# Attention on one core: VectorE adds the finished output projection to the result before it gates the next turn's first values

## The reference, cut to what matters

```python
q = _rope(jnp.einsum('bsd,hdp->bhsp', x, Wq))
k = _rope(jnp.einsum('bsd,hdp->bhsp', x, Wk))
gv = _gate(x, Wsel_v)                                   # sigmoid scores, the top 2 of 8 experts kept
v = jnp.einsum('bsd,bhse,hedp->bhsp', x, gv, Wv)
att = jax.nn.softmax(jnp.einsum('bhsp,bhtp->bhst', q, k) / np.sqrt(P), axis=-1)
o = jnp.einsum('bhst,bhtp->bhsp', att, v)
go = _gate(x, Wsel_o)
return jnp.einsum('bhsp,bhse,hepd->bsd', o, go, Wo)
```

## Time and profile before

| what | value |
|---|---|
| median of 3 runs | 3919.82 us (3918.64 to 3920.61) |
| the profiled execution's own time | 3914.3 us |
| its span, first to last instruction | 3912.5 us |
| mean granted TensorE clock, share of full speed | 0.980 |
| PE busy | 3596.8 us, 92% of the span |
| DVE busy | 3211.4 us, 82% |
| POOL busy | 2722.2 us, 70% |
| ACT busy | 2037.4 us, 52% |
| the sum into `acc`, 64 times | first starts at 1168.2 us, last at 3648.2 us |

### The profile page before, as it was taken

The page is one execution under the profiler, slowest core; times in us unless marked ns, Lnnn a source line. Parts: engine busy times, 40 slices in busy tenths (PEclk is TensorE's granted clock), DMA queues, the critical chain, the costliest instruction groups (busy, mean ns, idle before and its releaser), DMA issues. The chain is left out here.

```text
span 3912.5 us, 55524 instructions
## 1 busy us (share of the span) xinstructions
PE 3596.8 (92%) x15792; PEld 2472.4 (63%) x15792; DVE 3211.4 (82%) x3580; ACT 2037.4 (52%) x3795; POOL 2722.2 (70%) x2852
## 2 busy tenths in 40 slices
PE   6999999998669999999999999999999999999797
PEld 3444444444247777777777777777777777777586
DVE  6999989998748888888888887888887888888697
ACT  5666666666334454445454545444444445444455
POOL 4877788787657676677777677767677767776344
PEclk9999999999979999999999999999999999999898
DMA  2110111011043242323232323233323332222111
GB/s 78 54 49 27 65 70 71 20 56 60 25 159 81 56 110 55 81 60 105 55 87 78 77 64 100 60 76 89 76 60 77 88 73 68 66 70 68 43 33 49
DMA packets 76054, 267.78 MB, mean 68 GB/s; under 512 B 9326, under 2 KB 38894, under 8 KB 53072
## 3 DMA queue, kind: packets, MB, share of 16 engines
q1 hardware_dynamic: 74944, 262.83, 24.8%
q0 software_dynamic: 1040, 4.19, 0.3%
HBM read 247.85 MB, written 19.14 MB: 68 GB/s over the span
## 5 line engine op out<-in xcount | busy, mean ns | idle before, releaser
L384 POOL TENSOR_TENSOR state<-state,c_rows 128x1024 f32<-128x1024 f32 x256 | 604.6, 2365 | 215.1 <-DVE state L848 212.7
L848 DVE TENSOR_TENSOR_SCAN state<-dA,ps_a 128x1024 f32<-128x1024 f32 x256 | 585.2, 2286 | 46.8 <-PE ps_a L524 21.8
L1104 POOL TENSOR_TENSOR qk_full<-vg 128x512 f32<-128x512 f32 x256 | 330.1, 1289 | 254.3 <-DVE vg L1489 254.1
L715 ACT ACTIVATE dA<-dt,a_neg 128x511 f32<-128x511 f32 x512 | 338.8, 714 | 311.4 <-DVE state L848 309.5
L1489 DVE TENSOR_TENSOR vg<-ps_b,gates 128x1024 f32<-128x1024 f32 x256 | 313.6, 1225 | 221.2 <-PE ps_b L1215 188.6
L524 PE MATMUL ps_a<-state,ident 128*128 128x512 f32 x1024 | 481.9, 593 | 0.4 <-POOL state L384 0.4
L1213 PE MATMUL ps_b<-ogT_high,wo_high 128*128 128x512 f32 x1024 | 415.6, 406 | 33.8 <-POOL ogT_low L1117 27.2
L1378 ACT ACTIVATE prob<-ps_b,negmax 128x512 f32<-128x512 f32 x512 | 343.6, 676 | 188.9 <-DVE negmax L1495 188.9
L1213 PE MATMUL ps_b<-wv_high,xT_high 128*128 128x512 f32 x1024 | 414.3, 405 | 3.8 <-POOL wv_low L1097 3.8
L1215 PE MATMUL ps_b<-ogT_high,wo_low 128*128 128x512 f32 x1024 | 408.2, 399 | 0.0
L1214 PE MATMUL ps_b<-ogT_low,wo_high 128*128 128x512 f32 x1024 | 405.9, 396 | 0.0
(11 more groups left out here) (245 smaller groups left out, 8449.9 us busy)
## 6 DMA issues: line engine op xcount, KB each, us to landing
ogT_low<-gates_scratch SPq DMA_DIRECT2D x128, 512.0 KB, 6.3
wide_high<-gates_scratch SPq DMA_DIRECT2D x128, 512.0 KB, 9.7
xT<-xT_scratch SPq DMA_DIRECT2D x65, 512.0 KB, 3.3
c_rows<-c_scratch SPq DMA_DIRECT2D x32, 1024.0 KB, 5.4
wv<-in_wv SPq DMA_DIRECT2D x8, 1024.0 KB, 11.5
wo<-in_wo SPq DMA_DIRECT2D x8, 1024.0 KB, 13.5
x_in<-in_x SPq DMA_DIRECT2D x8, 512.0 KB, 5.1
x_a<-in_x SPq DMA_DIRECT2D x8, 512.0 KB, 7.1
```

The source lines that it names most:

```text
L384: pool.tensor_tensor(state, state, c_rows[:, n, :].unsqueeze(1).to_broadcast([P, HALF, S]), ALU.mult).then_inc(hc_done, 1)
L715: act.activation(dA[s % RING][:, m, 1:S], dt[par][:, HALF * f + m, 1:S], ACT.Exp, scale=a_neg[:, HALF * f + m, n:n + 1]).then_inc(dA_done, 1)
L848: dve.tensor_tensor_scan(h[s % RING][:, :, :].rearrange("p c s -> p (c s)"), dA[s % RING][:, :, :].rearrange("p c s -> p (c s)"), ps[:, DB ...
L1104: pool.tensor_tensor(v4[:, at, :, :], vg[:, at, 0:4, :], vg[:, at, 4:8, :], ALU.add).then_inc(vsum_done, 1)
```

## The change

The sum moves in front of the next turn's first `gate_values` on VectorE. Nothing else changes: no instruction is added or removed, and the operands, buffers and semaphores are the same.

```diff
                 if more_pairs:
                     tops(*coming, 3)
-                if more:
-                    gate_values(it + 1, j, b + 1, 0)
                 dve.wait_ge(acc_loaded, 16)
                 dve.wait_ge(out_psum, CREDIT + it * KD + KD)
                 dve.tensor_tensor(acc[:, bass.ds(b, 1), :, :], acc[:, bass.ds(b, 1), :, :], ps[:, OUT:OUT + KD, :].unsqueeze(1),
                                   ALU.add).then_inc(acc_done, 1)
+                if more:
+                    gate_values(it + 1, j, b + 1, 0)
```

## The result

| | before | after |
|---|---|---|
| median | 3919.23 us of 4 runs (3917.91 to 3920.61) | 3886.43 us of 4 runs (3884.64 to 3888.26) |
| ratio | | 0.992, interval 0.9908 to 0.9932 |
| profiled execution, span | 3914.3, 3912.5 us | 3888.26, 3886.4 us |
| mean granted clock | 0.980 | 0.976 |

3886 was forecast, with a range of 3880 to 3897.

A forecast was written before the change was run, and what follows sets the result against it. The prediction took TensorE's work and its gaps to bound the kernel. Closing 56 looped-boundary gaps of 0.61 us gives 34.2 us, so 3919.8 - 34.2 = 3885.6, rounded to 3886 us, with a range of 3880 to 3897.

The forecast's parts named there:

- What bounds a turn: Whole turn: as long as TensorE's work and its gaps, 39.00 us; other engines have 7 us or more to spare.
- When the sum starts: VectorE at a looped boundary: the sum starts 0.54 us after the last projection's start, between 0.43 and 0.63.
- When the transposes start: TensorE at a looped boundary: gate transposes start 0.33 us after the last scores' start, as between pairs.
- rival 2: Looped boundary: transposes' first load can't start before the last scores end; gain 0.47 us each, 26 in all, 3894; chance 0.06.
- The gain of one boundary: TensorE's gap at each looped boundary closes: 0.54 to 0.62 us, taken as 0.61.
- What becomes late: After the moved sum: gating, maxima, exponentials and GpSimd's value sum come later, all covered, thinnest by 0.13 and 0.18 us.
- The cover of the exponentials: ScalarE's exponentials before row block 3's scores load weights: 0.18 us to spare; beyond it each microsecond of lateness costs 56.
- A sign that misled: Profile after: some 56 waits of the scores (L1248) for the exponentials would appear if the maxima's lateness matters.
- The sum: Whole kernel: 56 looped boundaries times 0.61 us, 34.2 us gained; turns between pairs stay as they are.
- rival 4: Later in the turn: waits for low probabilities or low outputs give the gain back; about 3920 us; chance 0.07.
- rival 6: Looped boundary: VectorE's saved 0.45 us wait and ScalarE's earlier copy add a tenth; 40 us in all, 3880; chance 0.03.
- Rival 3: Row block 3's scores: exponentials up to 0.2 us late, leaving 0.41 us each, 23 in all, 3897 us; chance 0.10.

The follow-up runs named there:

- old_order_plus_06: Kernel before plus one unused VectorE maximum (128x512) between first gating and sum in each of 56 looped turns; 3953.44 us, ratio 1.0097 to the kernel before.
- ahead_of_sum_06: Changed kernel plus one unused VectorE maximum (128x512) in front of the sum's wait in each of 56 looped turns; 3885.36 us, ratio 0.9922 to the kernel before.
- last_pair_only: Kernel before with the sum moved ahead of the gating only in the 7 looped turns of the last pair of heads; 3910.52 us, one run.
- high_first: Changed kernel with the high-part products first in each turn's first output projection, only the others waiting for GpSimd's low part; 3868.34 us, ratio 0.9871 to the kernel before.
- late_maxima_03: Changed kernel plus one unused VectorE maximum (128x256) behind the first gating in each of 56 looped turns; 3886.41 us, ratio 0.9916 to the kernel before.

## Why the prediction was right

- **What bounds a turn.** TensorE's work and its gaps: shown by old_order_plus_06, ahead_of_sum_06 and last_pair_only for the changed boundary and by high_first for another gap.
- **When the sum starts.** 0.54 us after the last projection, bounded by 0.43 and 0.63. Measured 0.55.
- **When the transposes start.** 0.33 us after the last scores from the earlier trace rows; measured 0.35. The later start by the matmuls' modelled end, rival 2 with 0.47 us a boundary, did not come: the boundary gained 0.61. The load starts at 2418.67, and the last scores' row ends at 2418.75; that end is modelled, so this alone would be weak. The rule of the Trainium skill's page "TensorE: Matmul & The Clock Gate", Part 3, which gave the same, is not borne out by these rows.
- **The gain of one boundary.** 0.61 us; measured 34.1 / 56 = 0.61, between the two kernels with the gap filled.
- **What becomes late.** The maxima start 2.82 us after the last projection's start (2419.57 - 2416.75); 2.81 was worked out (2428.88 - 2426.07). The second gating and GpSimd's value sum cost nothing, as said. VectorE is idle for 0.23 us ahead of the second gating (0.13 forecast) and GpSimd for 1.08 ahead of its second value sum (1.07 forecast). The cover of the exponentials was mis-sized: 0.18 us forecast, 0.25 for the load by the rows of the trace after, and 0.38 for the turn. I took VectorE's 0.15 us for ScalarE's way to TensorE, which is 0.05, and left out that a load runs ahead of its matmul. It was on the safe side, and the price behind the cover, one for one, was right.
- **A sign that misled.** The prediction took 56 waits of the scores for the exponentials as the sign that lateness matters. They are in the view, and the turn doesn't pay for them: the releaser's name changed, not the gap.
- **The sum.** 34.2 us forecast and 32.8 measured between medians. The gain of the boundaries came out whole (34.1 us). What the sum put at nothing is the turn between pairs ("stays"): the eighth turns vary with the clock by up to 2 us each, and in these traces they lost some 4 us more with the change. The medians fall short of 34.2 in all three comparisons: 32.8 here, 32.4 for late_maxima_03 and 30.6 for ahead_of_sum_06, whose looped turns are those of the changed kernel. The boundary was forecast by its mechanism; that the median was met to within 1 us is in part luck. The gain was 1.4 us short, the median before came out 0.6 us under the one that I started from, and the runs of after lie 3.6 us apart.
- **The rivals.** The gain was not given back (rival 4), since the waits for the low probabilities stayed (the weight loads' 141.9 us for 382 waits became 141.6), and those for the low outputs too (27.2 us became 27.8). The 0.45 us that VectorE used to wait for GpSimd's gates brought nothing beyond TensorE's gap (rival 6). Rival 3 did not come, since the cover was wider than worked out.

## What to carry to other kernels

When one engine must end a result that the bounding engine waits for, look at what stands ahead of that operation on the helping engine at the moment the input is ready. Work there is paid in full, while the same work behind the result is free as long as its own users have cover. Work out the cover of each user from the trace with the handoff of the very pair of engines, count the head start that a weight load has on its matmul, and compare turn lengths in the trace, not single executions, when the gain is under one per cent. Look at the other turns as well: a gap that the change doesn't touch can cost more once the turns around it are shorter.

## What the runs showed of the hardware

- A gap of 2.78 us in TensorE's work was followed, in some of the pairs, by 2 to 6 us with matmuls 0.43 us apart in place of 0.23 (a granted clock of 0.92 over a window of 41 us with the longest). With the gap filled by 12 unused matmuls the window read 1.00 and the seven turns were alike to 0.03 us. With the gap cut to 1.43 to 1.48 us (high_first) shorter spells were left in three of seven pairs.
- A load of weights for all 128 rows starts while a matmul on the same rows is in flight: L1215's load and the matmul L1214 both at 2425.84.
- In the stream a load runs 0.23 us ahead of its matmul, and a load late by 0.08 us of that cost nothing (late_maxima_03).
- Handoffs differ by pair of engines: 0.15 us from the end of VectorE's sum (2428.45) to TensorE's transposes before the change, 0.12 to their weight load at 2428.57 in the same trace, and 0.05 us from the end of ScalarE's accumulator read to TensorE's weight load (2427.09 to 2427.14, 2500.79 to 2500.84).
